# Attention weighed four heads at a time, 512 columns wide, in pieces of four key blocks

## Chip, cores and metric

The kernel runs on one core of a Trainium2 chip. The metric is the time of one execution on the device, in microseconds (us), the median of several.

## The reference, cut

One post-norm layer: attention with 16 query heads on 4 key heads over 2048 tokens, then a mixture of 64 experts. Only the attention matters here.

```
x: (1, 2048, 512); H, HKV, HD = 16, 4, 128;  G = H // HKV = 4
q = rope((x @ Wq + bq).reshape(B, T, H, HD)); k, v alike with HKV heads
scores = einsum('bgjtd,bjsd->bgjts', q, k) * scale
wei = softmax(where(tril, scores, -inf))
out = einsum('bgjts,bjsd->bgjtd', wei, v)
x = layernorm(x + out @ Wo + bo)
... # then the experts
```

For each of the 4 key heads j there are 4 query heads g, and for each of them 16 query blocks of 128 tokens. Query block b sees b + 1 key blocks.

## The kernel before

The program has stages one after the other: projection (`stage_project`), attention (`stage_attend`), output projection, norm and routing (`stage_route`), then the experts. Each engine has its own program, written out by hand in Python loops, and engines wait for each other only by semaphores; each engine works strictly in the order in which its program is written. All operands of the large matmuls are kept as two halves, high (`h`, HI) and low (`l`, LO), and a product takes three matmuls (`split3`: lo x hi, hi x lo, hi x hi).

In attention a *unit* u is one query block of one head: u = 0..63 within a key head j, four units (g = 0..3) for each block b = u // 4. I call the four units of one query block a *row*, and name it by its number of key blocks, 1 to 16. Step i of an engine's program does:

- TensorE (PE), `scores`, L674: the scores of unit i into PSUM tile `S`, which has two groups of 1024 columns. Units of up to 8 key blocks use one group, alternating; wider units use both: group 0 (called S0 here) and group 1 (S1). A group may be overwritten when its former content has been through exp (`exped`). For narrow units the mask is added by a small bf16 matmul, L676.
- VectorE (DVE), `row_max` L808 (for S1 behind the mask, L806, and followed by L812), and `recip` (L819 or L821 and L824) for the unit before.
- ScalarE (ACT), `exp` L755, from `S` into `prob`, with a row sum; GpSimd (POOL), L870, scales `prob` by the reciprocal.
- `turn`, L686, on PE: transposes up to four 128x128 blocks of `prob` of unit i - LAG (3) into PSUM tile `TP` (two buffers). ScalarE copies `TP` into the high half `pTh` (`p_hi`, L764), VectorE subtracts and writes the low half `pTl` (`p_lo`, L830); then the `TP` buffer is free.
- `weigh`, L709, on PE: the values `v` times the halves of a *pair* of units (two heads, 256 columns), accumulated in PSUM tile `O`, at unit i - WEIGH (5). A pair's key blocks are spread over the steps of its two units, and it waits for the low halves four blocks at a time.
- `out_hi` L770 on ScalarE and `out_lo` L836 on VectorE split `O` into `oT`, and SyncE stores it to `o_scratch` (L603).

Within a step ScalarE does: out_hi, the first two high halves, exp of group 0, the other high halves, exp of group 1. VectorE does: out_lo, the maximum of group 0, the reciprocal, the first two low halves, the maximum of group 1, the other low halves. The buffers: `prob` 5, `pT` 2 (one for each pair, all 16 blocks), `TP` 2, `O` 2, `oT` 2.

## Time and profile before

| | |
|---|---|
| time, median of 3 runs | 2107.64 us (2106.67 to 2107.74) |
| the profiled execution | 2108.76 us, span 2106.9 us |
| PE busy | 2070.5 us, 98% |
| DVE, ACT, POOL busy | 80%, 66%, 41% |
| attention, first score to last weighing | about 286 to 1351 us |

The span is the time between the first and last instruction of the profiled execution; some 1.9 us lie around it. Busy shares of PE count modelled ends of pipelined matmuls, so the length of a series of matmuls divided by their number tells more than the mean duration of one.

### The profile page before, as it was taken

What the parts mean: (1) busy time and instruction counts of PE and PEld (TensorE: products, weight loads), DVE (VectorE), ACT (ScalarE), POOL (GpSimd) and SP (SyncE); (2) the same over time, 40 slices, a digit from 0 to 9 for tenths busy, and PEclk for the clock granted to TensorE, in tenths of its full rate; (3) what the DMA queues carried; (4) which work ended last, traced back from release to release, by engine and by line L of the source; (5) the groups of instructions that cost most, each with busy time, mean ns of one, the idle gap of its engine ahead of it and who ended that gap; (6) DMA issues with size and microseconds to landing.
All of it is one profiled execution on the core that took longest, in us unless ns stands there. A gap on an engine that the chain in (4) does not pass through costs nothing.

```text
span 2106.9 us, 39556 instructions
## 1 busy us (share of the span) xinstructions
PE 2070.5 (98%) x13605; PEld 1843.0 (87%) x13605; DVE 1677.1 (80%) x3566; ACT 1395.6 (66%) x2790; POOL 858.6 (41%) x813
## 2 busy tenths in 40 slices
PE   9999999999999999999999999999989999999998
PEld 7888878999889998899988899988878999999996
DVE  5899987887678876788767888656667888898886
ACT  3677776766667666676656766533446777777775
POOL 1000013333233332333323333245556777778774
PEclk9999999999999999999999999999999999999999
DMA  7557563110331103311053110478748999999997
GB/s 252 190 211 278 218 220 126 69 63 21 126 125 66 66 21 126 126 66 66 21 180 131 66 66 21 144 252 288 245 139 238 300 294 301 297 296 297 299 290 260
DMA packets 139635, 361.28 MB, mean 171 GB/s; under 512 B 16336, under 2 KB 33232, under 8 KB 134864
## 3 DMA queue, kind: packets, MB, share of 16 engines
q1 hardware_dynamic: 111376, 292.03, 39.4%
q0 software_dynamic: 28096, 67.12, 13.3%
q8 instruction: 97, 1.59, 0.3%
q14 instruction: 66, 0.54, 0.1%
HBM read 224.21 MB, written 134.89 MB: 170 GB/s over the span
## 4 chain that ended last, share of the span: by engine, by line
PE 79%; ACT 2%; DMA 2%; DVE 2%; issue 1%; POOL 0%; SPq 0%; DVEq 0%; ACTq 0%; POOLq 0%
PE p_S L674 18%; PE p_O L709 17%; PE p_TP L686 11%; PE p_pgu L1522 9%; PE p_acc L1064 8%; PE p_prest L1522 4%; PE p_py L1539 4%; PE p_tp L1508 3%; PE p_py L1540 1%; PE p_py L1541 1%; ACT p_prob L755 1%; DMA o_scratch<-p_oT 1%; PE p_lg L1086 1%; DMA qk_scratch<-p_qout 1%; ACT p_pT1h L764 0%
## 5 line engine op out<-in xcount | busy, mean ns | idle before, releaser
L674 PE MATMUL p_S<-p_kT,p_q 128*128 128x512 f32 (+3 forms) x1920 | 472.4, 376 | 9.8 <-ACT p_prob L755 9.3
L870 POOL TENSOR_SCALAR p_prob<-p_prob,p_inv 128x128 f32<-128x128 f32 (+7 forms) x256 | 191.2, 747 | 452.6 <-DVE p_inv L819 452.6
L674 PEld LDWEIGHTS p_S<-p_kT,p_q 128*128 128x128 f32 x1920 | 322.5, 189 | 60.7 <-ACT p_prob L755 16.5
L870 POOL TENSOR_SCALAR p_prob<-p_prob,p_inv,p_part 128x1024 f32<-128x1024 f32 x128 | 153.0, 1195 | 483.5 <-DVE p_inv L824 483.5
L686 PE MATMUL p_TP<-p_ident,p_prob 128*128 128x128 f32 x2176 | 303.1, 274 | 2.4 <-DVE p_pT1l L830 2.1
L686 PEld LDWEIGHTS p_TP<-p_ident,p_prob 128*128 128x128 f32 x2176 | 244.1, 140 | 31.0 <-issue 18.0
L808 DVE TENSOR_REDUCE p_nmax<-p_S 128x1 f32<-128x1024 f32 (+7 forms) x256 | 253.2, 989 | 20.8 <-PE p_S L674 15.2
L764 ACT CAST p_pT0h<-p_TP 128x512 fp32r<-128x512 f32 (+3 forms) x320 | 155.0, 527 | 134.5 <-PE p_TP L686 134.1
L764 ACT CAST p_pT1h<-p_TP 128x512 fp32r<-128x512 f32 (+3 forms) x320 | 154.7, 526 | 128.7 <-PE p_TP L686 128.1
L1796 POOL DMA_INDIRECT sum_scratch<-p_y,p_tokT x124 | 206.6, 1666 | 42.6 <-issue 36.6
L709 PE MATMUL p_O<-p_pT0h,p_v 128*128 128x256 f32 x1088 | 222.6, 288 | 0.2 <-DVE p_pT0l L830 0.2
L709 PE MATMUL p_O<-p_pT1h,p_v 128*128 128x256 f32 x1088 | 221.4, 288 | 0.1
L830 DVE TENSOR_TENSOR p_pT1l<-p_TP,p_pT1h 128x512 fp32r<-128x512 f32 (+3 forms) x320 | 181.5, 601 | 42.1 <-ACT p_pT1h L764 40.6
L830 DVE TENSOR_TENSOR p_pT0l<-p_TP,p_pT0h 128x512 fp32r<-128x512 f32 (+3 forms) x320 | 181.4, 600 | 33.0 <-ACT p_pT0h L764 32.8
L755 ACT ACTIVATE p_prob<-p_S,p_nm 128x128 f32<-128x128 f32 (+7 forms) x256 | 189.5, 740 | 18.4 <-DVE p_nm L808 16.9
L1784 POOL DMA_INDIRECT p_xg<-x_scratch,p_tokT x128 | 170.3, 1331 | 73.5 <-issue 37.2
L709 PEld LDWEIGHTS p_O<-p_pT0h,p_v 128*128 128x128 f32 x1088 | 177.7, 190 | 1.1 <-issue 0.4
L709 PEld LDWEIGHTS p_O<-p_pT1h,p_v 128*128 128x128 f32 x1088 | 177.4, 190 | 1.0 <-issue 0.3
L1064 PE MATMUL p_acc<-p_woh,p_ot 128*128 128x512 f32 x512 | 172.5, 402 | 0.0
L755 ACT ACTIVATE p_prob<-p_S,p_nmax 128x1024 f32<-128x1024 f32 x128 | 144.1, 1126 | 28.1 <-DVE p_nmax L808 27.8
L709 PE MATMUL p_O<-p_pT0l,p_v 128*128 128x256 f32 x544 | 153.4, 282 | 0.0
L709 PE MATMUL p_O<-p_pT1l,p_v 128*128 128x256 f32 x544 | 153.4, 282 | 0.0
(342 smaller groups left out, 4660.6 us busy)
## 6 DMA issues: line engine op xcount, KB each, us to landing
p_w_raw<-in_gu SPq DMA_DIRECT2D x64, 768.0 KB
qk_scratch<-p_qout SPq DMA_DIRECT2D x80, 512.0 KB, 2.8
p_q<-qk_scratch SPq DMA_DIRECT2D x16, 2048.0 KB, 9.3
o_scratch<-p_oT SPq DMA_DIRECT2D x128, 256.0 KB, 2.1
p_ot<-o_scratch SPq DMA_DIRECT2D x32, 1024.0 KB, 7.4
p_w_raw<-in_gu SPq DMA_DIRECT2D x64, 256.0 KB
v_scratch<-p_vout SPq DMA_DIRECT2D x16, 512.0 KB, 3.2
p_t_raw<-in_dn SPq DMA_DIRECT2D x32, 256.0 KB
```

The source lines that it names most:

```text
L674: mm = nc.tensor.matmul(out, x, y, start=(n == 0), stop=(n == 2))
L686: mm = nc.tensor.transpose(TP[n % 2][:, s % 4, :], prob[u % KEEP][:, s * P:(s + 1) * P], ident[:])
L709: mm = nc.tensor.matmul(O[p % 2][:], x, y, start=(s == 0 and n == 0), stop=(s == nb - 1 and n == 2))
L755: nc.scalar.activation(prob[k][:, a * 1024:a * 1024 + w], S[:, score_group(u, a), 0:w], ACT.Exp, bias=top[:, k:k + 1], accum_out=rsum[:, k ...
L764: nc.scalar.copy(pT[p % 2][HI][:, 4 * t:4 * t + m, u % 2, :], TP[n % 2][:, 0:m, :]).then_inc(turn_hi, 1)
L808: r = nc.vector.reduce_max(out[:, k:k + 1], S[:, score_group(u, a), 0:w], AX_X, negate=True)
L830: nc.vector.tensor_tensor(pT[p % 2][LO][:, 4 * t:4 * t + m, u % 2, :], TP[n % 2][:, 0:m, :], pT[p % 2][HI][:, 4 * t:4 * t + m, u % 2, :].b ...
L870: nc.gpsimd.tensor_scalar(prob[k][:, cols], prob[k][:, cols], inv[:, k:k + 1], scale, ALU.mult, ALU.mult).then_inc(normed, 1)
L1064: mm = nc.tensor.matmul(acc[k][:], a, w, start=(n == 0 and m == 0), stop=(n == H - 1 and m == 2))
L1522: mm = nc.tensor.matmul(out, a[:, col:col + P], b[:, d, :], start=(m == 0 and d == 0), stop=(m == 2 and d == NC - 1))
L1784: nc.gpsimd.indirect_dma_start(out=xg[k][c][:], out_offset=None, in_=x1_d, in_offset=bass.IndirectOffsetOnAxis(ap=tokT[:, e, c:c + 1], axi ...
L1796: nc.gpsimd.indirect_dma_start(out=sum_d[k], out_offset=bass.IndirectOffsetOnAxis(ap=tokT[:, e, c:c + 1], axis=0), in_=y[k][c][:], in_offs ...
```

## The change

The four heads of a row (a *quad* f) are weighed together, 512 columns wide: half as many weighing matmuls. The halves `pT` hold no longer 16 blocks of a pair but one *piece*, up to four key blocks of all four heads, in two buffers. Each row is cut into pieces t = 0..3; a turn (m, g) is piece m of head g, and below (t, g) names piece t of the row and head g. The turns of a row, piece by piece and head by head in a piece, are spread evenly over four steps, five steps behind the scores (`TURN`). Behind each turn of a piece stands at most one block's weighing of the piece before it (`turn_and_weigh`): a piece of four blocks is weighed behind all four turns of the next piece, a piece of one block only behind the last. `O` and `oT` become 512 wide, so that 64 outputs are split and stored instead of 128, and `prob` has 8 buffers instead of 5. The loop over key heads is now one run of 256 units. The lines that go from `weigh` on stand in the listing above and are left out of the diff.

```diff
     U = NB * G
-    blk = lambda u: u // G
+    ALL = HKV * U
+    QUADS = ALL // G
+    HEAD_QUADS = U // G
+    blk = lambda u: u % U // G
     width = lambda u: (blk(u) + 1) * P
     ngrp = lambda u: 1 if width(u) <= 1024 else 2
-    ntr = lambda u: -(-(blk(u) + 1) // 4)
-    SG = [0]
-    TG = [0]
-    for u in range(U):
-        SG.append(SG[-1] + ngrp(u))
-        TG.append(TG[-1] + ntr(u))
-    PAIRS = U // 2
-    KEEP = 5
-    LAG = 3
-    WEIGH = LAG + 2
-    OUT = WEIGH + 2
+    nblk = lambda f: f % HEAD_QUADS + 1
+    npieces = lambda f: -(-nblk(f) // 4)
+    SG = [0, *itertools.accumulate(ngrp(u) for u in range(ALL))]
+    PG = [0, *itertools.accumulate(npieces(f) for f in range(QUADS))]
+    PIECE = [(f, t) for f in range(QUADS) for t in range(npieces(f))]
+    HEAD_GROUPS, HEAD_PIECES = SG[U], PG[HEAD_QUADS]
+    KEEP = 8
+    TURN = 5
+    FREE = 2
+    STEPS = ALL + TURN
 
...
+    def turns(i):
+
+        if i < TURN:
+            return []
+        f, k = divmod(i - TURN, G)
+        n = npieces(f)
+        return [(PG[f] + r // G, r % G) for r in range(k * n, (k + 1) * n)]
+
+    def in_piece(m):
+        f, t = PIECE[m]
+        return min(4, nblk(f) - 4 * t)
+
+    def out_step(f):
+
+        return f * G + TURN + G + 1 + (3 // npieces(f + 1) if f + 1 < QUADS else 0)
+
+    OUT = {out_step(f): f for f in range(QUADS)}
+    LAST_OUT = out_step(QUADS - 1)
 
...
         prob = [sb(f"prob{k}", [P, T], kb=51 + 8 * k) for k in range(KEEP)]
-        pT = [[sb(f"pT{k}{s}", [P, NB, 2, P], F32R) for s in "hl"] for k in range(2)]
-        oT = [sb(f"oT{k}", [P, 2, 2, P], F32R) for k in range(2)]
-        k_next = sb("k_next", [P, 2, 512], F32R)
+        pT = [[sb(f"pT{k}{s}", [P, 4, G, P], F32R) for s in "hl"] for k in range(2)]
+        oT = [sb(f"oT{k}", [P, G, 2, P], F32R) for k in range(2)]
+        assert sb.end <= 159 * 1024
+        k_next = sb("k_next", [P, 2, 512], F32R, kb=159)
         v_next = sb("v_next", [P, 4, 2, HD], F32R)
         assert sb.end == 167 * 1024
...
         S = ps("S", [P, 2, 1024])
         TP = [ps(f"TP{k}", [P, 4, P]) for k in range(2)]
-        O = [ps(f"O{k}", [P, 2, P]) for k in range(2)]
+        O = [ps(f"O{k}", [P, G, P]) for k in range(2)]
...
-            def store(j, p):
-                b, g = blk(2 * p), 2 * p % G
-                sp.wait_ge(o_lo, j * PAIRS + (p + 1 + FREE))
-                sp.dma_start(o_d[b, :, bass.ds(j, 1), g:g + 2].rearrange("p o g h t -> p (o g) h t"),
-                             oT[p % 2][:].bitcast(F32)).then_inc(o_out[p % 2], 16)
+            def store(j, b):
+                sp.wait_ge(o_lo, j * HEAD_QUADS + (b + 1 + FREE))
+                sp.dma_start(o_d[b, :, bass.ds(j, 1)].rearrange("p o g h t -> p (o g) h t"),
+                             oT[b % 2][:].bitcast(F32)).then_inc(o_out[b % 2], 16)
 
...
-            def turn(j, back, u, t):
-                if t % 2 == 0:
-                    pe.wait_ge(normed, j * SG[U] + (SG[u] + t // 2 + 1 - back * SG[U]))
-                n = TG[u] + t
-                pe.wait_ge(turn_lo, j * TG[U] + (n + 1 - back * TG[U]))
-                for s in range(4 * t, min(4 * t + 4, blk(u) + 1)):
-                    mm = nc.tensor.transpose(TP[n % 2][:, s % 4, :], prob[u % KEEP][:, s * P:(s + 1) * P], ident[:])
+            def turn(m, g):
+                f, t = PIECE[m]
+                u = f * G + g
+                pe.wait_ge(normed, SG[u] + t // 2 + 1)
+                pe.wait_ge(turn_lo, m * G + g + 1)
+                for n in range(in_piece(m)):
+                    s = 4 * t + n
+                    mm = nc.tensor.transpose(TP[g % 2][:, n, :], prob[u % KEEP][:, s * P:(s + 1) * P], ident[:])
                 mm.then_inc(turned, 1)
 
...
+            def weigh(m, n):
+                f, t = PIECE[m]
+                s = 4 * t + n
+                if s == 0:
+                    if f == 0:
                         pe.wait_ge(v_in0, 16)
...
+                    elif f % HEAD_QUADS == 0:
+                        pe.wait_ge(v_first, f // HEAD_QUADS)
+                    pe.wait_ge(o_lo, f + 1)
+                elif s % 4 == 0 and f % HEAD_QUADS == s:
+                    pe.wait_ge(v_in[s // 4], f // HEAD_QUADS * 16 + 16)
+                if n == 0:
+                    pe.wait_ge(turn_lo, m * G + G + FREE)
+                for i, (x, y) in enumerate(split3([v[:, s, h, :] for h in (HI, LO)],
+                                                  [pT[m % 2][h][:, n, :, :] for h in (HI, LO)])):
+                    mm = nc.tensor.matmul(O[f % 2][:], x, y, start=(s == 0 and i == 0),
+                                          stop=(s == nblk(f) - 1 and i == 2))
+                if n == in_piece(m) - 1:
+                    mm.then_inc(weighed, 1)
+
...
+            def turn_and_weigh(m, g):
+                turn(m, g)
+                n = g - (G - in_piece(m - 1)) if m > 0 else -1
+                if n >= 0:
+                    weigh(m - 1, n)
+
+            def step(i):
+                todo = turns(i)
+                if i < ALL:
+                    scores(i, 0)
+                if i == 1:
+                    keep_busy(nc, 20, S[:, 0, 512:512 + P], ident)
+                for m, g in todo[0:2]:
+                    turn_and_weigh(m, g)
+                if i < ALL and ngrp(i) == 2:
+                    scores(i, 1)
+                for m, g in todo[2:]:
+                    turn_and_weigh(m, g)
 
             pe.wait_ge(own.mask_ready, 2)
...
+            for i in range(STEPS):
+                step(i)
+            for n in range(in_piece(len(PIECE) - 1)):
+                weigh(len(PIECE) - 1, n)
+            pe.wait_ge(exped, SG[ALL])
 
...
+            def p_hi(m, g):
+                act.wait_ge(turned, m * G + g + 1)
+                if g == 0:
+                    act.wait_ge(weighed, m + 1)
+                n = in_piece(m)
+                nc.scalar.copy(pT[m % 2][HI][:, 0:n, g, :], TP[g % 2][:, 0:n, :]).then_inc(turn_hi, 1)
+
+            def out_hi(f):
+                act.wait_ge(weighed, PG[f + 1] + FREE)
+                if f >= 2:
+                    act.wait_ge(o_out[f % 2], 16 * (f // 2))
+                nc.scalar.copy(oT[f % 2][:, :, HI, :], O[f % 2][:]).then_inc(o_hi, 1)
+
+            def step(i):
+                if i in OUT:
+                    out_hi(OUT[i])
+                todo = turns(i) if i < STEPS else []
                 for a in range(2):
...
+                    for m, g in todo[2 * a:2 * a + 2]:
+                        p_hi(m, g)
+                    if i < ALL and a < ngrp(i):
+                        exp(i, a)
+
+            for i in range(LAST_OUT + 1):
+                step(i)
+                if ALL < i <= ALL + len(between):
+                    between[i - ALL - 1](act)
 
...
+            def step(i):
+                if i % U == 0 and 0 < i < ALL:
+                    take_k(i // U)
+                if i % U == TURN - 1 and U < i < ALL:
+                    take_v(i // U)
+                if i in OUT:
+                    out_lo(OUT[i])
+                todo = turns(i) if i < STEPS else []
+                if i < ALL:
+                    row_max(i, 0)
+                if 1 <= i <= ALL:
+                    recip(i - 1)
+                for m, g in todo[0:2]:
+                    p_lo(m, g)
+                if i < ALL and ngrp(i) == 2:
+                    row_max(i, 1)
+                for m, g in todo[2:]:
+                    p_lo(m, g)
+
+            for i in range(LAST_OUT + 1):
+                step(i)
+                if ALL + 1 < i <= ALL + 1 + len(between):
+                    between[i - ALL - 2](dve)
 
```

How TensorE's order changes while a 9-block row is scored and the row before it, of 8 blocks, is turned. `p_prob` is the softmax weights, 101 to 108 its buffers, `p_kT` and `p_q` are keys and queries, `p_S` the scores, and behind [waits ..] stand the semaphores waited for. Before, in this kind of step:

```order
L674 MATMUL p_S<-p_kT,p_q_99 128x512 [waits p2_exped]
L674 MATMUL p_S<-p_kT,p_q_99 128x512 x5
L686 MATMUL p_TP<-p_ident,p_prob_101 128x128 [waits p2_turn_lo,p2_normed]
L686 MATMUL p_TP<-p_ident,p_prob_101 128x128 x3
L686 MATMUL p_TP<-p_ident,p_prob_101 128x128 [waits p2_turn_lo]
L686 MATMUL p_TP<-p_ident,p_prob_101 128x128 x3
L674 MATMUL p_S<-p_kT,p_q_99 128x128 [waits p2_exped]
L674 MATMUL p_S<-p_kT,p_q_99 128x128 x2
L709 MATMUL p_O<-p_pT0h,p_v 128x256 [waits p2_turn_lo,p2_o_lo]
```

and with the change:

```order
L690 MATMUL p_TP<-p_ident,p_prob_107 128x128 x3
L708 MATMUL p_O<-p_pT1h,p_v 128x512
L708 MATMUL p_O<-p_pT1l,p_v 128x512
L708 MATMUL p_O<-p_pT1h,p_v 128x512
L690 MATMUL p_TP<-p_ident,p_prob_108 128x128 [waits p2_turn_lo,p2_normed]
L690 MATMUL p_TP<-p_ident,p_prob_108 128x128 x3
L708 MATMUL p_O<-p_pT1h,p_v 128x512
L708 MATMUL p_O<-p_pT1l,p_v 128x512
L708 MATMUL p_O<-p_pT1h,p_v 128x512
L677 MATMUL p_S<-p_kT,p_q_99 128x128 [waits p2_exped]
L677 MATMUL p_S<-p_kT,p_q_99 128x128 x2
L677 MATMUL p_S<-p_kT,p_q_99 128x512 [waits p2_exped]
```

The two turns of the unit (eight transposes in a row, then S1, then all weighing of the step) become a turn and one block's weighing, twice, with S1 and then the next unit's S0 directly behind the last weighing.

TensorE again, while a 10-block row is scored. Before, a step with three turns (the third stands behind the weighing, below the rows shown):

```order
L686 MATMUL p_TP<-p_ident,p_prob_101 128x128 [waits p2_turn_lo,p2_normed]
L686 MATMUL p_TP<-p_ident,p_prob_101 128x128 x3
L686 MATMUL p_TP<-p_ident,p_prob_101 128x128 [waits p2_turn_lo]
L686 MATMUL p_TP<-p_ident,p_prob_101 128x128 x3
L674 MATMUL p_S<-p_kT,p_q_99 128x256 [waits p2_exped]
L674 MATMUL p_S<-p_kT,p_q_99 128x256 x2
L709 MATMUL p_O<-p_pT0h,p_v 128x256 [waits p2_turn_lo]
L709 MATMUL p_O<-p_pT0l,p_v 128x256
L709 MATMUL p_O<-p_pT0h,p_v 128x256 x2
L709 MATMUL p_O<-p_pT0l,p_v 128x256
L709 MATMUL p_O<-p_pT0h,p_v 128x256 x2
```

and with the change, in the second of the four steps in which the 9-block row is turned:

```order
L690 MATMUL p_TP<-p_ident,p_prob_104 128x128 [waits p2_turn_lo,p2_normed]
L690 MATMUL p_TP<-p_ident,p_prob_104 128x128 x3
L708 MATMUL p_O<-p_pT1h,p_v 128x512
L708 MATMUL p_O<-p_pT1l,p_v 128x512
L708 MATMUL p_O<-p_pT1h,p_v 128x512
L690 MATMUL p_TP<-p_ident,p_prob_101 128x128 [waits p2_turn_lo,p2_normed]
L690 MATMUL p_TP<-p_ident,p_prob_101 128x128 x3
L708 MATMUL p_O<-p_pT0h,p_v 128x512 [waits p2_turn_lo,p2_o_lo]
L708 MATMUL p_O<-p_pT0l,p_v 128x512
L708 MATMUL p_O<-p_pT0h,p_v 128x512
L677 MATMUL p_S<-p_kT,p_q_99 128x256 [waits p2_exped]
L677 MATMUL p_S<-p_kT,p_q_99 128x256 x2
```

Before, the weighing behind the turns is of a pair turned two steps earlier. With the change the turn of `p_prob_104`, the last of piece 0, is followed by one weighing of the row before, by the first turn of piece 1, and then by the first weighing of piece 0, which waits for `turn_lo`.

VectorE, from an output split to the mask of group 1, before:

```order
L836 TENSOR_TENSOR p_oT_110<-p_O,p_oT_110 128x2x128 [waits p2_o_hi]
L808 TENSOR_REDUCE p_nmax<-p_S 128x1 [waits p2_scored]
L821 SCALAR_TENSOR_TENSOR p_den<-p_rsum,p_part 128x1 [waits p2_exped]
L824 RECIPROCAL p_inv<-p_den 128x1 [waits p2_den_ready]
L830 TENSOR_TENSOR p_pT0l<-p_TP,p_pT0h 128x4x128 [waits p2_turn_hi] x2
L806 TENSOR_TENSOR p_S<-p_S,p_maskf 128x128 [waits p2_scored]
L808 TENSOR_REDUCE p_nmax_115<-p_S 128x1 [waits p2_max_part]
```

and with the change:

```order
L833 TENSOR_TENSOR p_oT_113<-p_O,p_oT_113 128x4x128 [waits p2_o_hi]
L807 TENSOR_REDUCE p_nmax<-p_S 128x1 [waits p2_scored]
L820 SCALAR_TENSOR_TENSOR p_den<-p_rsum,p_part 128x1 [waits p2_exped]
L823 RECIPROCAL p_inv<-p_den 128x1 [waits p2_den_ready]
L828 TENSOR_TENSOR p_pT1l<-p_TP,p_pT1h 128x4x128 [waits p2_turn_hi] x2
L805 TENSOR_TENSOR p_S<-p_S,p_maskf 128x128 [waits p2_scored]
```

The order within a step is the same, and the output is four heads wide.

## Rows read from the trace of the kernel before

**Rows 1.** The page: busy time of each engine over the span.

```profile
PE 2070.5 (98%) x13605; PEld 1843.0 (87%) x13605; DVE 1677.1 (80%) x3566; ACT 1395.6 (66%) x2790; POOL 858.6 (41%) x813
```

**Rows 2.** The windows view of attention: engines' busy us, instructions, clock, DMA.

```profile
286.00:1351.00 1065.00, 1052.39 (x7534) 954.76 (x7533) 840.05 (x1810) 715.27 (x1673) 341.06 (x384) 1.00 0.25 85
```

**Rows 3.** Groups by form, PE: count, busy us, mean ns, idle before.

```profile
L674 PE MATMUL p_S<-p_kT,p_q 128*128 128x512 f32 x1344 | 376.2, 407 | 3.6 <-ACT p_prob L755 3.0
L686 PE MATMUL p_TP<-p_ident,p_prob 128*128 128x128 f32 x2176 | 303.1, 274 | 2.4 <-DVE p_pT1l L830 2.1
L709 PE MATMUL p_O<-p_pT0h,p_v 128*128 128x256 f32 x1088 | 222.6, 288 | 0.2 <-DVE p_pT0l L830 0.2
L709 PE MATMUL p_O<-p_pT1h,p_v 128*128 128x256 f32 x1088 | 221.4, 288 | 0.1
...
L709 PE MATMUL p_O<-p_pT0l,p_v 128*128 128x256 f32 x544 | 153.4, 282 | 0.0
L709 PE MATMUL p_O<-p_pT1l,p_v 128*128 128x256 f32 x544 | 153.4, 282 | 0.0
...
L674 PE MATMUL p_S<-p_kT,p_q 128*128 128x384 f32 x192 | 46.2, 348 | 3.9 <-ACT p_prob L755 3.9
...
L674 PE MATMUL p_S<-p_kT,p_q 128*128 128x256 f32 x192 | 34.6, 289 | 1.5 <-ACT p_prob L755 1.5
L674 PE MATMUL p_S<-p_kT,p_q 128*128 128x128 f32 x192 | 31.0, 271 | 0.9 <-ACT p_prob L755 0.9
L676 PE MATMUL p_S<-p_maskb,p_identb 128*128 128x128 bf16 x128 | 29.5, 230 | 0.0
...
L106 PE MATMUL p_S<-p_ident 128*128 128x128 f32 x40 | 4.7, 276 | 0.0
```

**Rows 4.** The chain that ended last, merged: start us, us, what.

```profile
1344.39 0.87 PE p_TP L686 x8
...
1345.26 5.76 PE p_O L709 x48
...
1369.22 4.17 PE p_acc L1064 x18
...
1425.20 3.53 PE p_acc L1064 x15
```

**Rows 5.** The same chain, from 889 to 894 us.

```profile
889.33 1.66 PE p_S L674 x6
890.99 0.45 PE p_TP L686 x4
...
891.46 1.07 ACT p_pT1h L764 x2
892.54 1.11 ACT p_prob L755 x2
...
893.69 0.50 PE p_S L674
```

**Rows 6.** Timelines of PE, DVE, ACT and DVE: start, us, instructions [idle before].

```profile
709.28 0.59 ACT L764 CAST p_pT1h<-p_TP 128x512 fp32r<-128x512 f32 x1 [1.22 <-PE p_TP L686]
...
709.90 0.69 DVE L830 TENSOR_TENSOR p_pT1l<-p_TP,p_pT1h 128x512 fp32r<-128x512 f32 x1 [0.31 <-ACT p_pT1h L764]
...
890.83 1.03 PE L686 MATMUL p_TP<-p_ident,p_prob 128*128 128x128 f32 x8
...
890.83 0.42 DVE L836 TENSOR_TENSOR p_oT<-p_O,p_oT 128x256 fp32r<-128x256 f32 x1 [0.97 <-ACT p_oT L770]
891.18 1.22 DVE L808 TENSOR_REDUCE p_nmax<-p_S 128x1 f32<-128x1024 f32 x1
...
892.63 1.27 DVE L830 TENSOR_TENSOR p_pT1l<-p_TP,p_pT1h 128x512 fp32r<-128x512 f32 x2
```

**Rows 7.** The chain that ended last, at 1083 us.

```profile
1083.07 10.02 DMA o_scratch<-p_oT
```

More of the change, by code:

```diff
@@ L553, in stage_attend @@
         o_out = [sem(f"o_out{k}") for k in range(2)]
-        FREE = 2
         def load_q(sp, j, tc):
@@ L573, in load_v @@
                          .rearrange("b o p h d -> (o p) b h d")).then_inc(v_in[c], 16)
-        def lagged(i, lag, first):
-            u = i - lag
-            return (u, 0) if u >= 0 else None if first else (u + U, 1)
-        def steps(eng, step, tail, between={}):
-            for j in range(HKV):
-                for i in range(U):
-                    step(j, i, j == 0)
-            for i in range(U, U + tail + 1):
-                step(HKV - 1, i, False)
-                for piece in between.get(i, []):
-                    piece(eng)
         def first_k(sp):
```

196 lines of the change are left out of this document (51 added, 145 removed).

## The prediction

> **What bounds the kernel now.** The page first: one core, and PE is busy for 98% of the span [rows 1]. The edit touches only attention, so the stretch from its first score to its last weighing is read next: 286 to 1351 us, clock 1.00, which is the upper level of 2.4 GHz, PE at 1052 of 1065 [rows 2]. A busy PE is not PE at its peak, because the ends of pipelined matmuls are modelled, so I went from durations to intervals in the chain of waits [rows 4]: 48 weighing matmuls, 256 wide, take 5.76 us, 120 ns each; 8 turns take 0.87 us, 109 ns each; 512-wide matmuls take 4.17 us for 18 (232 ns) or 3.53 us for 15 (235 ns). The counts are in [rows 3]: scores 1344 x 232 ns = 311.8; 192 each of 384, 256 and 128 wide, at an estimated 176 (midway), 120 and 109 ns, 77.8; 128 masks at some 66 ns, 8; turns 2176 x 109 = 237.2; weighing 3264 x 120 = 391.7; 40 fillers, 4.4. The sum is 1031 us against 1065. So TensorE's own rate bounds attention, and some 34 us are waits. Reading each step (from one first score group to the next, less its instructions) I place about 7.5 us of them in each head: 3.1 in rows of up to 4 key blocks, 2.9 in those of 9 to 11, 1.5 in those of 14 to 16; the rest is the start and one late store.
>
> How such a wait comes about is seen in the 9-block rows [rows 5]: the next S group may start only when ScalarE has taken exp of the last, and ScalarE's queue puts two high halves (`p_hi`) ahead of that exp. From the end of S at 890.83 [rows 6] to the next S at 893.69 is 2.86 us: two turns, 0.2 to ScalarE, two copies (0.96), exp and its sum (1.2).
>
> **The change, part by part.**
>
> *Wider weighing.* 3264 matmuls of 120 ns become 1632 of 512 columns. At 232 ns that is 378.6, a gain of 13.1 us; at 235 it is 8.2. The rows of before hold no 512-wide weighing, but `p_S` and `p_acc` have its shape, so I take 13. The low end is 8; above, I grant 22 for an interval down to 226 ns. The Trainium skill (TensorE: Matmul & The Clock Gate, Back-to-back issue gap) gives N/2.4 + 2.5 ns for an isolated stream, 109 and 216 ns here; by it the gain would be an estimated 4 us. The rows show 120 and 232, so the trace differs and decides. The weight loads halve, but PEld ran under the matmuls; turns keep their count and their 109 ns.
>
> *Fewer, wider outputs.* `out_hi` and `out_lo` run 64 times, 512 wide, instead of 128 times, 256 wide. ScalarE and VectorE are hidden on average, so nothing by throughput. The buffer of a stored output is now reused eight steps later: the wait behind the store that landed after 10.02 us [rows 7] goes, -1.9 us by my reading of that step.
>
> *The order of turns and weighings.* This decides. Before, weighing lagged two steps behind turning, over all 16 blocks of halves; now the halves hold two pieces, TensorE alternates turn and weighing, and a piece is weighed directly behind its last turn. Prices from [rows 6]: a turn of four ends 0.44 us after its start; +0.2 to ScalarE; VectorE starts 0.62 after ScalarE and takes 0.69; +0.07 back to PE (an estimate; from exp's end to the next S it is 0.04 in [rows 5]). So a low half is there 1.58 us after its turn's end at best. On VectorE it also stands behind the row maximum: the maximum starts 0.2 after the S group ends (taken like ScalarE's), the low half some 1.46 behind it (891.18 to 892.63), at 1.67, and it is there at 2.43. Counting from the end of the first S group, three matmuls (0.70) per weighing, in each head:
>
> (a) Steps with two turns and two score groups (five: rows of 7 and 8 blocks turned while 9- and 10-block rows are scored). Order: turn, weigh, turn, weigh, S1, S0. The second turn ends at 1.57, is copied until 2.25, exp to 3.45, so the next S starts at 3.52. PE would be there at about 2.63 (1.93 where a weighing is missing, against 2.83). 0.9 each, 4.4 us.
>
> (b) Rows of 9 to 12 blocks, three pieces, second step: turn (0,3), weigh, turn (1,0), weigh piece 0. PE reaches that weighing at 1.57; the low half of (0,3) is there at 2.43. 0.87 lost in the 9- and 12-block rows, 1.15 in the 10- and 11-block rows, where VectorE comes late from (d). 4.0 us.
>
> (c) Their third step: VectorE first waits for `out_hi`, which stands behind an exp, then takes the maximum; piece 1's last half is late by 0.83, 0.6, 0.35, 0. 1.8 us.
>
> (d) First step after a row whose last piece was short (rows of 10, 11, 14, 15): no weighing stands between the turns; the third turn waits for TP until 2.43 but PE is there at 1.40, 1.56, 2.09, 2.26. 1.03 + 0.87 + 0.5 (two turns late) + 0.2 = 2.6 us.
>
> (e) Output ahead of the maximum in rows of 13 to 16: 0.2 each, 0.8 us. (f) Rows of up to 4 blocks: VectorE's maximum, reciprocal and low half (0.95 to 1.5 us a step) exceed PE where no weighing falls, as before: 3.1 us. (g) Rows of 5 to 8 otherwise: 0.2.
>
> Sum 16.9 a head against 7.5 now: +9.4, times four +37.6 us. What is queued behind: every wait is on TensorE itself, so all that follows moves. Waits (a) to (e) lie on the engine that sets the end and nothing covers them.
>
> *The tail.* After the last score there are no S groups between pieces. From a piece's last turn to its weighing PE has 0.70 + 0.44 = 1.14 us against 1.58: 0.45 for each of four pieces, 0.9 more before the last. The output projection's weights are cast between, and push halves back; the last store is twice as large. I take +5, bounds +2 and +9.
>
> **Sum.** -13.1 - 1.9 + 37.6 + 5 = +27.6 us. The profiled execution took 2108.76 us, 1.1 above the median of 2107.64, so by the run it is 2136.4 and on the scale of the median 2135. The waits are walked, each from a fresh step; a wait once paid may spare the next, so I bound them by two thirds of 16.9 (11.3 - 7.5 = +3.8 a head, 15 us in all, sum +5) and four thirds (22.5 - 7.5 = +15 a head, 60 us, sum +50). The likeliest case's own range: 2112 to 2158.
>
> **Rivals.**
>
> *R1, the halves are ready when asked for: faster.* If the first wait of a row shifts VectorE and ScalarE enough ahead that (a) to (d) fall to the 2.9 us of today, a head has 7.0 us: 4 x -0.5 = -2, and the sum is -13.1 - 1.9 - 2 + 5 = -12: 2096. It turns from loss to gain where the new waits per head fall under 2.5 us above today's (10.0/4). For it: PE waits little today and both other engines have slack (VectorE 840, ScalarE 715 of 1065 [rows 2]). Against: the waits in [rows 5] are chains, not loads, and recur in every step today although those engines have that slack. 14%.
>
> *R2, it cancels (within 0.2%, about 4 us, which is what a measurement of this kernel can tell from no change).* Waits of +2.5 a head, as if only (a) and part of (b) came. 2108. 7%.
>
> *R3, the chain feeds itself.* In the three-piece rows and the small ones `out_lo` waits for `out_hi`, the maximum for `out_lo`, exp for the maximum, S for exp: if each of the 64 outputs costs a further 0.6 us (one 512-wide copy), +38 more: 2173. For it: today VectorE already idles 1.0 us before an output [rows 6]. Against: the outputs are half as many. 9%.
>
> *R4, the wide matmul costs clearly less than two narrow ones.* To pay for waits and tail (40.7 us) it would need (391.7 - 40.7) / 1632 = 215 ns. At one column per cycle of 2.4 GHz, the clock in [rows 2], 512 columns take 213 ns: a gain of 44 us, 2104. Against: the 512-wide streams in [rows 4] run at 232 to 235 ns. 1%. The Trainium skill's same section also gives about 131 ns per 512-wide matmul for a sustained stream; by that the estimated gain would be 178 us. The trace's 232 ns contradicts it.
>
> **How the numbers follow.** The likeliest case, waits of the walked size, holds 69%; R1 14, R2 7, R3 9, R4 1. Of the 69 nothing lies under 2112. Faster 0.15 (R1, R4), same 0.07, slower 0.78. For a range with 8 in 10 I leave out most of R1 and of R3: 2103 to 2158. Predicted 2135.
>
> **What would show it.** Right: weighing at about 232 ns for three-matmul groups (0.70 us); a wait of weighing for `p_pTl` that is absent today, in rows of 9 to 12 blocks; S waiting for `p_prob` with steps of about 4.9 us (today 4.36) while rows of 9 blocks are scored; TP waiting for `p_pTl` at the first step of rows 10, 11, 14; attention some 1092 us long, and the stages after it unchanged in length. Wrong: attention at or under 1060 us; or waits before S in the rows of 13 to 16 blocks, which I take as nearly free; or an interval of weighing far from 232 ns. What would upset it most is a step order on VectorE or ScalarE that I read wrongly, since (a) to (d) all rest on who stands behind whom.

## The result, and the profile after

The changed kernel takes 2149.62 us (median of 4 runs, 2148.39 to 2150.7) against 2107.15 us for the kernel before beside it: 1.0198 times, 95% interval 1.0185 to 1.0211. It is slower by 42 us (whether by more than 2% the interval leaves open), where I forecast +27.6 (2135, range 2103 to 2158). Its profiled execution took 2150.70 us, span 2148.6.

The page of the kernel after: span, busy time of the engines, and the head of the chain.

```profile
span 2148.6 us, 36176 instructions
...
PE 2067.0 (96%) x11973; PEld 1747.7 (81%) x11973; DVE 1683.3 (78%) x3502; ACT 1415.1 (66%) x2726; POOL 858.9 (40%) x813
...
PE 72%; DVE 7%; ACT 4%; DMA 1%; issue 1%; POOL 0%; SPq 0%; POOLq 0%; ACTq 0%; DVEq 0%
```

1632 matmuls fewer than in [rows 1], and yet a longer span; VectorE, all but absent from the chain before (2%), holds 7% of it. The windows view of attention, now until 1391 us (columns as in [rows 2]):

```profile
286.00:1391.00 1105.00, 1047.90 (x5903) 857.99 (x5902) 847.42 (x1747) 734.91 (x1610) 340.94 (x384) 1.00 0.24 82
```

Attention, from its first score to the first matmul behind it, is 1103.7 us long (286.9 to 1390.6) instead of 1063.9: +39.8 of the +41.6 in the span. The other 1.9 lie behind it (756.1 us became 758.0). The clock is 1.00 in both, DMA is light, and VectorE and ScalarE have more room than before, so nothing became scarce: TensorE does less and waits more. The view of waits in attention, TensorE's rows (us in total, times, longest; one wait can be in both engines' rows, so they are not added):

```profile
PEld p_S L677 <- ACT p_prob L750: 34.1, 37, 1.5
PE p_S L677 <- ACT p_prob L750: 26.6, 33, 1.3
...
PE p_O L708 <- DVE p_pT1l L828: 8.3, 17, 0.8
PE p_O L708 <- DVE p_pT0l L828: 6.7, 10, 0.8
PEld p_S L677 <- DVE p_kT L788: 5.4, 3, 1.8
PE p_TP L690 <- DVE p_pT0l L828: 5.3, 12, 0.8
...
PE p_TP L690 <- DVE p_pT1l L828: 4.4, 8, 0.9
PE p_S L677 <- DVE p_kT L788: 4.1, 3, 1.4
```

Before, the same view had S waiting for `p_prob` 9.3 us in 18 waits, TP for `p_pT1l` 2.1, O for `p_pT0l` 0.2. Weighing (L708) waits for a low half 27 times where it waited once: the kind of wait that the forecast named.

To split work from waiting I use the measure of the forecast, step by step: the time from one first score group to the next, less the intervals of the step's instructions (231 ns for 512 columns, 176 for 384, 120 for 256, 109 for 128, 64 for a mask). Over attention the intervals fall by 14.7 us (some 1029.6 to 1014.9) and the waits rise from 34.2 to about 88.7: -14.7 + 54.5 = +39.8. A later head takes 273.7 us instead of 263.8, and waits 21.1 instead of 7.5. The waits of the second key head, by the terms of the forecast; steps are numbered 0 to 63 by the unit scored:

| term | steps: measured wait, us | forecast | measured |
|---|---|---|---|
| (a) two turns, two score groups | 32 to 36: 0.82, 1.06, 1.03, 1.02, 0.99 | 4.4 | 4.9 |
| (b) second step, three pieces | 38, 42, 46, 50: 0.97, 1.09, 0.97, 0.97 | 4.0 | 4.0 |
| (c) third step, behind an output | 39, 43, 47, 51: 0.70, 0.65, 0.64, 0.41 | 1.8 | 2.4 |
| (d) no weighing between turns | 41, 45, 57, 61: 1.03, 0.93, 0.58, 0.25 | 2.6 | 2.8 |
| (e) output in rows of 13 to 16 | 53 to 55, 58: 0.01 to 0.09 | 0.8 | 0.1 |
| (f) rows of up to 4 blocks | 0 to 15, of these step 10: 1.51, step 14: 1.34 | 3.1 | 4.7 |
| (g) rows of 5 to 8 | 16 to 31 | 0.2 | 0.4 |
| not forecast: the next head | 63: 1.54 | 0 | 1.5 |

Some of them in the trace. (a), the chain that ended last, steps 34 and 35 (start us, us, what):

```profile
636.49 1.66 PE p_S L677 x6
638.14 0.44 PE p_TP L690 x4
638.58 0.69 PE p_O L708 x3
639.27 0.45 PE p_TP L690 x4
...
639.75 0.59 ACT p_pT0h L758
640.33 1.11 ACT p_prob L750 x2
...
641.49 1.64 PE p_S L677 x6
```

From S to S are 5.00 us (4.9 forecast). Scoring, turn, weigh and turn run into one another; then TensorE hands over to ScalarE, which copies the second turn ahead of the exp that frees S. The three weighing matmuls take 0.69 us: 231 ns each.

(b), PE's timeline of step 46 (idle before an instruction, and its releaser, in brackets):

```profile
700.26 0.60 PE L690 MATMUL p_TP<-p_ident,p_prob 128*128 128x128 f32 x4
700.61 0.48 PE L708 MATMUL p_O<-p_pT1h,p_v 128*128 128x512 f32 x1
...
701.39 0.60 PE L690 MATMUL p_TP<-p_ident,p_prob 128*128 128x128 f32 x4
702.74 0.47 PE L708 MATMUL p_O<-p_pT0h,p_v 128*128 128x512 f32 x1 [0.75 <-DVE p_pT0l L828]
```

A turn of four takes 0.44 us, so the one at 701.39 is done by 701.83; the weighing behind it starts 0.9 later, because the low half made from the turn before it stands behind maximum and reciprocal:

```profile
700.46 1.22 DVE L807 TENSOR_REDUCE p_nmax<-p_S 128x1 f32<-128x1024 f32 x1 [0.56 <-PE p_S L677]
701.60 0.21 DVE L820 SCALAR_TENSOR_TENSOR p_den<-p_rsum,p_part 128x1 f32<-128x1 f32 x1
701.84 0.16 DVE L823 RECIPROCAL p_inv<-p_den 128x1 f32<-128x1 f32 x1
701.92 0.67 DVE L828 TENSOR_TENSOR p_pT0l<-p_TP,p_pT0h 128x512 fp32r<-128x512 f32 x1
```

The two long waits of (f), here step 14 in the chain. The output stands ahead of the maximum in VectorE's step 13, exp waits for that maximum, and the scores two units on wait for that exp; step 10 has the same, from the output in step 9:

```profile
579.52 0.69 DVE p_oT L833
580.21 0.61 DVE p_nm L807
...
580.84 0.79 ACT p_prob L750 x2
...
581.67 0.96 PE p_S L677 x3
```

And the wait that I had not forecast, at the end of the second head, in the chain:

```profile
812.77 1.24 DVE p_nmax L807
...
814.03 0.16 DVE p_nm L811
814.19 1.20 DVE p_pT0l L828 x2
815.39 0.61 DVE p_kT L788
...
816.04 0.55 PE p_S L677 x3
```

`take_k` is the first thing of VectorE's step 0 and stands behind the two low halves of step 63. The next head's scores wait for it.

### The profile page after: what moved, and what is told of

Same layout as the page of the kernel before. It is cut to its first block, busy times and chain, and to the rows that moved or that the text cites. A ratio compares the mean times of both kernels' runs of the same rounds, so it can differ in the third digit from the quotient of the medians.

```text
span 2148.6 us, 36176 instructions
## 1 busy us (share of the span) xinstructions
PE 2067.0 (96%) x11973; PEld 1747.7 (81%) x11973; DVE 1683.3 (78%) x3502; ACT 1415.1 (66%) x2726; POOL 858.9 (40%) x813
## 3 DMA queue, kind: packets, MB, share of 16 engines
q8 instruction: 85, 1.39, 0.3%
## 4 chain that ended last, share of the span: by engine, by line
PE 72%; DVE 7%; ACT 4%; DMA 1%; issue 1%; POOL 0%; SPq 0%; POOLq 0%; ACTq 0%; DVEq 0%
PE p_S L677 16%; PE p_O L708 15%; PE p_TP L690 9%; PE p_acc L1062 8%; PE p_pgu L1520 8%; PE p_prest L1520 4%; PE p_py L1537 4%; DVE p_nmax L807 3%; PE p_tp L1506 3%; ACT p_prob L750 2%; PE p_py L1538 1%; PE p_py L1539 1%; DVE p_pT0l L828 1%; DVE p_pT1l L828 1%; DVE p_oT L833 1%
## 5 line engine op out<-in xcount | busy, mean ns | idle before, releaser
L677 PEld LDWEIGHTS p_S<-p_kT,p_q 128*128 128x128 f32 x1920 | 343.6, 188 | 106.7 <-ACT p_prob L750 34.1
L690 PE MATMUL p_TP<-p_ident,p_prob 128*128 128x128 f32 x2176 | 337.8, 273 | 11.1 <-DVE p_pT0l L828 5.3
L758 ACT CAST p_pT0h<-p_TP 128x512 fp32r<-128x512 f32 (+2 forms) x320 | 171.1, 544 | 157.2 <-PE p_TP L690 156.4
L708 PE MATMUL p_O<-p_pT0h,p_v 128*128 128x512 f32 x576 | 248.6, 436 | 7.0 <-DVE p_pT0l L828 6.7
L708 PE MATMUL p_O<-p_pT1h,p_v 128*128 128x512 f32 x512 | 222.1, 436 | 8.3 <-DVE p_pT1l L828 8.3
L828 DVE TENSOR_TENSOR p_pT0l<-p_TP,p_pT0h 128x512 fp32r<-128x512 f32 (+2 forms) x320 | 195.9, 629 | 21.0 <-ACT p_pT0h L758 17.8
L708 PEld LDWEIGHTS p_O<-p_pT0h,p_v 128*128 128x128 f32 x576 | 108.7, 189 | 25.9 <-issue 8.9
L807 DVE TENSOR_REDUCE p_nm<-p_S 128x1 f32<-128x128 f32 (+7 forms) x128 | 96.3, 753 | 36.2 <-PE p_S L679 36.1
L708 PEld LDWEIGHTS p_O<-p_pT1h,p_v 128*128 128x128 f32 x512 | 96.6, 189 | 25.0 <-issue 7.7
L1365 POOL TENSOR_SCALAR p_lo_hot<-p_iota_lo,p_lo 128x128 f16<-128x128 f32 x120 | 79.0, 677 | 90.2 <-DVE p_hi L1290 90.2
```

The lines of the kernel that those rows point to most:

```text
L677: mm = nc.tensor.matmul(out, x, y, start=(n == 0), stop=(n == 2))
L690: mm = nc.tensor.transpose(TP[g % 2][:, n, :], prob[u % KEEP][:, s * P:(s + 1) * P], ident[:])
L708: mm = nc.tensor.matmul(O[f % 2][:], x, y, start=(s == 0 and i == 0), stop=(s == nblk(f) - 1 and i == 2))
L758: nc.scalar.copy(pT[m % 2][HI][:, 0:n, g, :], TP[g % 2][:, 0:n, :]).then_inc(turn_hi, 1)
L807: r = nc.vector.reduce_max(out[:, k:k + 1], S[:, score_group(u, a), 0:w], AX_X, negate=True)
L828: nc.vector.tensor_tensor(pT[m % 2][LO][:, 0:n, g, :], TP[g % 2][:, 0:n, :], pT[m % 2][HI][:, 0:n, g, :].bitcast(F32), ALU.subtract).then_ ...
```

## The experiments

My theory (W): TensorE waits at the named steps because of who stands behind whom in the engines' programs. A rival (V): the same work in fewer, larger instructions loads VectorE or ScalarE so that they set the pace, whatever the order. W says that moving instructions without changing the work takes the time back; V says that it does not. A second question is whether the wider matmul saves anything. Each "changed kernel" below is the one of the diff, 2149.62 us, and differences are between medians. The runs come in groups, with the kernel before beside each: 2107.55 us in that of e1 to e4, 2109.36 in that of e5 to e8, 2107.85 in that of e9 to e12, against 2107.15 beside the changed kernel. Taken against these, e5 to e8 come out 2.2 us lower than stated (+6.0, -14.3, -19.7, -32.0), the others by 0.4 to 0.7. Differences of about 4 us (e2, e4) are little more than this, and what is read from them rests on the steps in the trace.

**e1_narrow: the width alone undone.**

```diff
-                                                  [pT[m % 2][h][:, n, :, :] for h in (HI, LO)])):
-                    mm = nc.tensor.matmul(O[f % 2][:], x, y, start=(s == 0 and i == 0),
-                                          stop=(s == nblk(f) - 1 and i == 2))
+                                                  [pT[m % 2][h] for h in (HI, LO)])):
+                    for c in (0, 2):
+                        mm = nc.tensor.matmul(O[f % 2][:, c:c + 2, :], x, y[:, n, c:c + 2, :],
...
```

> The changed kernel, each 512-wide weighing issued as two 256-wide ones; order, buffers and waits stay. Theory W (the order makes waits, the width saves some 14 us): slower than the changed kernel by 9 to 14 us, 2159 to 2164, attention's waits a little smaller. Rival X (the wide matmul is what costs, by its length or its operand reads): back towards the kernel before, 2107 to 2130. Rival V (VectorE and ScalarE are simply too busy): no change, 2150, since their work is the same.

2156.13 us, 1.0229 [1.0212, 1.0246]: +6.5 on the changed kernel, under the 9 to 14 that I expected and the 14.7 of the intervals. Where TensorE does not wait the narrow form costs less than the intervals say (step 54: 6.98 us becomes 7.05, some 9.5 over attention), and waits pay the rest: weighing waits for low halves fall from 8.3 and 6.7 us to 6.9 and 6.5, S for `p_prob` on the load side from 34.1 to 32.0. The width does save, but only half of what its intervals promise counts here. The rival that the wide matmul is what costs (2107 to 2130) is out.

**e2_exp_first: in steps with two turns, exp ahead of the second high half.**

```diff
+                if i < ALL and ngrp(i) == 2 and len(todo) == 2:
+                    p_hi(*todo[0])
+                    exp(i, 0)
+                    p_hi(*todo[1])
+                    exp(i, 1)
+                    return
```

> The changed kernel, but in the five steps of each head with two turns and two score groups ScalarE takes exp of group 0 between the two high halves instead of behind both. Theory W: each of these steps loses its wait of about 1 us before the next S group; 20 steps, -16 to -19 us, 2131 to 2134, other steps unchanged. Rival V: the same work in another order, so no change, 2149 to 2151. Rival Y (the wait for S comes from VectorE's maximum): less than 4 us gained.

2145.66 us, 1.0181 [1.0164, 1.0198]: -4.0, a miss, at the edge of what rival Y of the expectation allows. Steps 32, 34 and 36 do what (a) says: 0.82, 1.03, 0.99 fall to 0.35, 0.33, 0.29. But step 33 keeps 0.91: no weighing stands between its turns, and maximum (from 633.56) and exp (from 634.82) alone last until the next scores at 636.08. Step 35 rises from 1.02 to 2.20. In these two steps the wait does come through VectorE's maximum, as rival Y says. The chain at step 35:

```profile
642.48 0.44 ACT p_prob L750 x2
642.92 0.48 ACT p_oT L764
...
643.43 0.69 DVE p_oT L839
644.12 1.14 DVE p_nmax L813
...
645.29 1.21 ACT p_prob L750 x2
...
646.54 1.66 PE p_S L677 x6
```

The exp of the second score group now ends later on ScalarE; `out_hi` stands behind it, `out_lo` behind that, and the maximum behind `out_lo`. One wait was exchanged for another.

**e3_out_late: VectorE's output behind its first maximum.**

```diff
-                if i in OUT:
-                    out_lo(OUT[i])
                 todo = turns(i) if i < STEPS else []
                 if i < ALL:
                     row_max(i, 0)
+                if i in OUT:
+                    out_lo(OUT[i])
```

> The changed kernel, but VectorE splits the output behind the maximum of group 0 instead of ahead of it. Theory W: VectorE no longer idles for ScalarE's output copy before the maximum. The third steps of rows of 9 to 12 blocks lose 0.3 to 0.7 us each, the two waits of 1.3 to 1.5 us a head in rows of 2 and 1 blocks mostly go: -3 to -4 us a head, 2134 to 2139. Rival V: 2149 to 2151.

2140.70 us, 1.0157 [1.014, 1.0174]: -8.9, most of what was expected (2134 to 2139). Step 10 falls from 1.51 to 0.56 (0.60 of it comes back in step 11), step 14 from 1.34 to 0.42, step 51 from 0.41 to nothing; 39 rises by 0.25. Steps 0 to 15 together fall from 4.7 to 3.4, against 3.1 forecast. So the excess of (f) is mostly the output ahead of the maximum.

**e4_recip_late: the reciprocal behind the first low halves.**

```diff
-                if 1 <= i <= ALL:
-                    recip(i - 1)
                 for m, g in todo[0:2]:
                     p_lo(m, g)
+                if 1 <= i <= ALL:
+                    recip(i - 1)
```

> The changed kernel, but VectorE takes the reciprocal of the former unit behind the first low halves instead of ahead of them (0.33 us). Theory W: each wait of weighing or turning for a low half in rows of 9 to 12 blocks, ten or eleven a head, is shorter by 0.3 us: -10 to -14 us, 2136 to 2140. Rival V: 2149 to 2151. If GpSimd's scaling, which comes later by it, is near the path, slower than the changed kernel.

2153.51 us, 1.0219 [1.0202, 1.0236]: +3.9, a miss in sign. Where I looked it worked: steps 38, 45, 46, 50, 57, 61 lose 0.24 to 0.34 each, the 0.30 us of the two small instructions; 41 to 43, aimed at too, do not fall. Elsewhere it cost more: step 35 +0.6, 62 +0.5, 63 +0.8. At step 35 the chain now runs through low half, `p_den`, `p_inv` (0.30 us that had been off it), mask, maximum, exp, output, maximum and exp. GpSimd, the rival in the expectation, is in neither chain that I read (steps 35 and 62 to 0); what lengthens step 62 stays open. And step 0 of the second and third head rose by 1.6 each, where no operand is late: its weighings take 1.28 and 1.08 us instead of 0.69. The windows of that place, e4 and then the changed kernel (columns as in [rows 2], the clock third from the end):

```profile
542.70:546.90 4.20, 4.20 (x17) 3.52 (x18) 1.32 (x3) 1.32 (x4) 0.00 (x0) 0.59 0.97 392
```

```profile
542.50:546.90 4.40, 4.40 (x28) 3.77 (x29) 2.26 (x6) 2.27 (x6) 2.29 (x2) 1.00 1.01 404
```

The granted clock was 0.59 over these 4.2 us, so mostly the lower level of 1.2 GHz, directly behind the wait for `take_k`, which had grown from 1.37 to 1.69 us of idle PE. Twice 1.6 is 3.2 of the 4.0 us that this profile's attention is longer; without it, e4 would lose little, and still not win.

**e5_front: a short piece weighed behind the first turns of the next, not the last** (rows over 8 blocks).

```diff
-                n = g - (G - in_piece(m - 1)) if m > 0 else -1
-                if n >= 0:
+                size = in_piece(m - 1) if m > 0 else 0
+                early = m > 0 and nblk(PIECE[m - 1][0]) > 8
+                n = g if early else g - (G - size)
+                if 0 <= n < size:
```

> The changed kernel, but the short last piece of a row of 9 or more blocks is weighed behind the first turns of the next row instead of behind the last ones, so that work stands between the turns of those first steps. Theory W: the third turn then comes later by 0.7 (one block) or 1.4 us (two blocks), so the waits of 1.03, 0.93 and 0.58 us in the first steps behind rows of 9, 10 and 13 blocks fall to about 0.3, 0 and 0; work is the same. -2.0 us a head, 2140 to 2143. Rival V: 2149 to 2151.

2157.78 us, 1.0232 [1.0215, 1.0249]: +8.2, a miss in sign. Steps 45 and 57 gain 0.8 and 0.6, as (d) says; 41, expected to fall to 0.3, keeps 0.97. But 42, 46, 50, 58, 62 and 2 rise by 0.7 to 1.0 each: the weighing that I moved forward, 0.7 us, had been what TensorE did while it waited for the next low half. In the waits, weighing for the low halves rises from 15.0 to 24.3 us, while TP falls from 9.7 to 3.4.

**e6_cut1: in the second step of a three-turn row, only one turn ahead of the second score group.**

```diff
+    def cut(i):
+        return 1 if i < ALL and ngrp(i) == 2 and len(turns(i)) == 3 and (i - TURN) % G == 1 else 2
...
-                for m, g in todo[0:2]:
+                for m, g in todo[:cut(i)]:
...
```

> The changed kernel, but in the second step of turning a row of 9 to 12 blocks all engines take group 1 behind the first turn instead of behind the second: the last turn of piece 0, a weighing, S1, the first turn of piece 1, the first weighing of piece 0. Theory W: the wait of that weighing for the low half (0.97, 1.09, 0.97, 0.97 us) shrinks by the length of S1, 0.35 to 1.0 us. -2 to -3 us a head, 2138 to 2142. Rival V: 2149 to 2151.

2137.52 us, 1.0138 [1.0121, 1.0155]: -12.1, slightly more than expected. Scores (0.7 us or more) now stand where TensorE waited for the low half: steps 38, 42, 46 and 50 go from 0.97, 1.09, 0.97, 0.97 to 0.63, 0.58, 0.31, -0.02, and 43, 47 and 51 fall by 0.2 to 0.4 more.

**e7_exp_out: e2 and e3 together.**

```diff
+                    p_hi(*todo[0])
+                    exp(i, 0)
+                    p_hi(*todo[1])
+                    exp(i, 1)
...
                     row_max(i, 0)
+                if i in OUT:
+                    out_lo(OUT[i])
```

> e2 and e3 together. In e2 four of the five steps of a head lost up to 0.7 us, but the step with an output gained a wait of 1.2 us: the output's copy came behind a later exp, and VectorE's maximum behind the output. With the output behind the maximum this should go. Theory W: -9 of e3, and -0.5, -0.15, -0.7, -0.7 and -0.7 us a head of e2, together 2128 to 2132. If the two do not interact: 2137 (the sum of their single gains, 4 and 9).

2132.12 us, 1.0109 [1.0092, 1.0126]: -17.5, as expected, where the two alone add up to -12.9. Step 35 is at 0.70. That shows the reading of e2: its lost gain was the output standing ahead of the maximum.

**e8_all: e3, e2, e5, e6, the reciprocal late only in three-turn steps, and `take_k` early.**

```diff
-                if i % U == 0 and 0 < i < ALL:
-                    take_k(i // U)
...
+                late = i < ALL and ngrp(i) == 2 and len(todo) == 3
...
+                if i % U == U - 1 and i < ALL - 1:
+                    take_k((i + 1) // U)
                 for m, g in todo[cut(i):]:
                     p_lo(m, g)
```

> All edits that shorten a wait, together: e3, e2, e5, e6; the copy of the next key head's first keys taken ahead of VectorE's last low halves instead of behind them (-1 us at each of three heads); and the reciprocal behind the first low halves only in steps with three turns (there e4 shortened waits by 0.3 us). Theory W: 2149.6 less 20 (e7), 8, 10, 3 and 5: 2100 to 2108, that is about the kernel before. Rival V: not under 2125, since no engine has less work than in the changed kernel.

2119.79 us, 1.0055 [1.0038, 1.0072]: a miss, though -30 us. Step 63 falls from 1.54 to 0.35, so `take_k` behind the low halves was its cause; but step 0 behind it rises from 0.09 to 0.61, so some 0.7 us is gained at each edge. Steps 46, 58, 62 and 2 stand at 0.92, 0.61, 0.78 and 1.01: e5's cost remains.

**e9_best: e8 without e5, the reciprocal late in first steps of four turns too.**

```diff
-                late = i < ALL and ngrp(i) == 2 and len(todo) == 3
+                late = i < ALL and ngrp(i) == 2 and (len(todo) == 3 or len(todo) == 4 and (i - TURN) % G == 0)
```

> e8 without the edit of e5, whose gain in first steps was given back in the next ones: there the weighing of the row before had stood between the last turn of piece 0 and the first weighing of piece 0. In exchange the late reciprocal also in first steps with four turns. Theory W, step by step from e8 and e6: steps 41 and 42 -0.4, 45 and 46 -0.4, 57 and 58 -0.3, 61 and 62 -0.6, 1 and 2 -0.2 us a head: -7 to -8 us against e8's 2119.8, 2111 to 2114, still above the kernel before. If e5 was right as part of the whole: 2125 or more.

2114.10 us (6 runs), 1.0031 [1.0019, 1.0044]: at the upper edge of what was expected, 35.5 us under the changed kernel with the same instructions of the same sizes. The waits, the same rows:

```profile
PE p_S L681 <- ACT p_prob L754: 10.3, 26, 0.8
PE p_O L712 <- DVE p_pT1l L838: 3.2, 13, 0.7
PE p_TP L694 <- DVE p_pT0l L838: 3.1, 8, 0.4
...
PE p_O L712 <- DVE p_pT0l L838: 0.6, 2, 0.4
PE p_S L681 <- DVE p_kT L798: 0.5, 3, 0.2
```

VectorE and ScalarE do all that they did in the changed kernel, in a shorter time. V is out.

**e10_best_narrow: e9 with the edit of e1.**

> e9 with each 512-wide weighing issued as two 256-wide ones. In e1 this cost 6.5 us, less than the 14 us of TensorE's own rate, by theory W because the steps that wait hide it. With fewer waits more of it must show: 8 to 12 us above e9, 2120 to 2125. If the width were worth only what e1 showed, 6 to 7 us.

2121.60 us, 1.0066 [1.0052, 1.008]: +7.5 on e9, just under what was expected. Even with few waits left, the narrow form costs half of what the intervals say; step 54 gives 7.04 us against 6.97.

**e11_before_out_late: the kernel before, with e3's edit.**

```diff
-                if at and i % 2 == OUT % 2:
-                    out_lo(j, at[1], at[0] // 2)
+                out = at if at and i % 2 == OUT % 2 else None
...
+                if out:
+                    out_lo(j, out[1], out[0] // 2)
```

> The kernel before, with VectorE's split of the output behind the maximum of group 0 instead of ahead of it (the edit of e3). Theory W: the same chain (exp, output copy, output low half, maximum) makes part of the kernel before's 7.5 us of waits a head, in rows of 1 to 4 and 14 to 16 blocks: -1 to -2 us a head, 2100 to 2104. If the chain matters only with 512-wide outputs: 2106 to 2109.

2105.92 us (11 runs, against 2107.85 in 22), 0.9992 [0.9983, 1.0001]: not told from no change. The trace has 0.2 to 0.4 us gone in steps 10, 35, 37 and 39 (S waits for `p_prob` 6.5 us instead of 9.3); the second and third head take 262.1 us each instead of 263.8, so 1.7 less. Four times that is 6.8 us, of the size that I expected, though not where I expected it: steps 52 to 59, in which rows of 14 and 15 blocks are scored, keep their 0.18 and 0.08 each. This profile's attention is indeed 4.3 us shorter than that of before (1059.6 against 1063.9), but it starts 1.8 us later (288.8 against 287.0), behind a stretch of the projection with a granted clock of 0.86 (10 to 22 us; 1.00 before). In the last head some of it is given back at the late store of [rows 7], the chain's longest piece there, here and in e12:

```profile
1080.30 11.15 DMA o_scratch<-p_oT
```

```profile
1085.47 11.35 DMA o_scratch<-p_oT
```

It lands 11.15 us after its issue instead of 10.02, so TensorE waits 4.4 us over steps 8 and 9 where before had 2.3 in step 8, and the granted clock is 0.77 to 0.80 around it. The last head takes 283.6 us instead of 282.9.

**e12_before_out_exp: e11 with exp ahead of the second high half in rows of 9 and 10.**

```diff
-                    for args in turns[2 * a:2 * a + 2]:
+                    for n, args in enumerate(turns[2 * a:2 * a + 2]):
+                        if n == 1 and a == 0 and i < U and blk(i) in (8, 9):
+                            exp(j, i, 0)
...
```

> e11, and ScalarE takes exp of group 0 between the two first high halves while rows of 9 and 10 blocks are scored (the edit of e2 in the kernel before, where both turns stand together). The S group may then start 2.66 us after the last one's end instead of 2.86: at most 0.2 us in 8 steps a head, -4 to -6 us below e11, 2095 to 2100, if VectorE's second low half, now later, is not missed.

2111.19 us (11 runs), 1.0013 [1.0004, 1.0022]: a miss, about 5 us slower than e11. Steps 37 and 39 rise from 0.02 to 0.56 and 0.46. They have three turns; the third needs the TP buffer of the first, and a wait of this form appears that e11 lacks:

```profile
PEld p_TP L686 <- DVE p_pT0l L832: 2.6, 8, 0.4
...
PEld p_TP L686 <- DVE p_pT1l L832: 1.2, 4, 0.3
```

And steps 33 and 34 gain nothing (0.34, 0.35 become 0.44, 0.44); which instruction holds them I did not trace, and it stays open. The second and third head take 263.3 us instead of e11's 262.1. The rest of the difference between the profiles lies in the last head's store and in the first head (256.4 us against 251.7), where another output store is late, behind a `qk_scratch` transfer of 10.62 us, and the clock is 0.79 from 306 to 314 us. My edit moves neither store, so of the 5 us I count 1 a head as its effect in this profile, and leave the rest to the stores.

## Why the forecast was right, and where it was short

*What bounds the kernel.* Right: TensorE's own rate, with waits made by order. Of the signs named in the forecast, the waits for `p_pTl`, the steps of 4.9 us and the interval of 231 ns came true; attention is 1103.7 us, not 1092. The experiments make this more than a reading, since e9 takes back 35.5 of 42 us by order alone.

*Wider weighing, -13.1.* The intervals say -14.7, since the wide one takes 231 ns where I had 232; R4 is out. But the term is not worth its face value: e1 and e10 put it at 6.5 and 7.5 us. Part of that is the seams: step 54 has four weighings and no wait, and takes 7.04 us in e10 and 6.97 in e9, 0.018 a weighing, 9.5 us over 544. The rest is eaten by waits, which start earlier when the work ahead of them is shorter.

*The late store, -1.9.* Right as far as one profile shows: no wait of this kind is in the chain of after. e11 and e12 show that its size in the kernel before is no constant: 10.02, 11.15 and 11.35 us from issue to landing.

*Waits, +37.6.* This is the term that was mis-sized. Waits in attention rose by 54.5; without the tail (4.4) and with the store's 1.9 back, the four heads have 52.0 more, against 37.6. The walked terms held ((b) exactly, (a) and (d) within 12%, (c) within a third), and e2, e3, e6 found each at its step. What failed is the sentence "rows of up to 4 blocks ... as before: 3.1 us": I carried the number of before over, though a 512-wide output now stands ahead of the maximum that steps 10 and 14 wait for, the very mechanism that I priced in (c). They cost 2.9 us a head; e3 takes 1.9 of it away, of which 0.6 comes back in step 11. The other lack is `take_k` at the head's edge (1.5 us, three times): the change part by part never asked what stands behind the last low halves of a head. (e), 0.8, was not there. Together: 0.5 + 0.6 + 0.2 - 0.7 + 1.6 + 0.2 + 1.5 = 3.9 a head, 14 us over four with one head's edge less; that is the difference.

*One reading of [rows 5]* does not add up: two turns, 0.2, two copies and exp are 3.2 us, not 2.86. The chain there has one turn of four (0.45) ahead of ScalarE, since the first copy runs beside the second turn. The sum does not use the figure.

*The tail, +5.* TensorE waits 4.4 us behind the last first score group, 4.1 more than before, and for the reason given. The chain there shows the turn, the hand-over to ScalarE and VectorE, and the weighing:

```profile
1380.82 0.45 PE p_TP L690 x4
...
1381.29 0.60 ACT p_pT0h L758
...
1381.91 0.70 DVE p_pT0l L828
...
1382.66 0.96 PE p_O L708 x3
```

From the turn's end to the weighing are 1.39 us, by [rows 6] 1.58 were forecast.

*Rivals.* R1 assumed that ScalarE's and VectorE's slack would make the halves ready; they kept their slack and were late. R2 needed new waits of 2.5 us a head; a later head has 13.6 more. R3, the chain that feeds itself, is there in small: e3 is worth 8.9 us over 64 outputs, 0.14 each, not 0.6.

*The clock.* Forecast at the upper level, and so it is, in all of the changed kernel's attention in windows of 4 us.

*Stages behind attention.* Forecast unchanged; 1.9 us longer. No experiment looked at this.

*No version of the new form beats the kernel before*: the best, e9, is 1.0031 [1.0019, 1.0044] of it. My reading, which no run tests by itself: pieces of four blocks leave TensorE one turn and one weighing between making a half and using it; two steps lay between them before.

## What to carry to other kernels

When engines run hand-ordered programs, a rate saved on the bounding engine is eaten by waits where the distance between making a value and using it becomes shorter than the chain that makes it; here 15 us of matmul time were bought with 54 us of waits while every other engine had slack. Walk every row of the new order, the small ones and the loop's edges too, and take no term over "as before" when the instruction in it has doubled. Before moving one instruction to shorten a wait, ask what it covered and who stands behind its new place: e2, e4, e5 and e12 each removed the wait they aimed at in some steps and made another elsewhere, which ate part of the gain in e2 and more than all of it in the others; e2 gave its gain only together with e3.
